# Both attentions' scores computed in row tiles of 64 partitions, rotated keys without a high and a low half, and projection jobs spread over more banks

## What is computed

```
# L0_attn: 16 heads of 8, causal, window 64, relative bias
attn = softmax(q @ k.T * 8**-0.5 + mask + bias);  x = LN(x + (attn @ v) @ w_proj.T + b)
# L0_xattn: 16 heads of 64 over the 512 context tokens
q = (LN(x) @ Wq) per head;  k, v = split(LN(ctx) @ Wkv) per head
k = [k1*cos - k2*sin, k2*cos + k1*sin]            # k1, k2: the two halves of a head's 64 features
attn = softmax(clip(q @ k.T * 64**-0.5, -11, 11)); x = LN(x + (attn @ v) @ Wo + bo)
```

## Time and profile before

| | us |
|---|---|
| Median of 3 runs (1313.61 to 1315.66) | 1315.2 |
| The profiled execution, its own time | 1313.62 |
| Its span | 1311.9 |
| PE busy in the span | 1029.7 (78%) |
| DVE busy | 894.7 (68%) |
| ACT busy | 672.8 (51%) |
| POOL busy | 644.1 (49%) |
| Mean granted TensorE clock | 0.915 |

### The profile page before, as it was taken

One profiled execution on the slowest core, in us unless ns is written; L12 is line 12 of the kernel. 1 busy time (PEld: TensorE's weight loads), 2 busy tenths in 40 slices (PEclk: granted clock), 3 DMA queues, 4 the chain that ended last, 5 costly groups with the idle time before them and its releaser, 6 DMA issues.

```text
span 1311.9 us, 18842 instructions
## 1 busy us (share of the span) xinstructions
PE 1029.7 (78%) x6723; PEld 667.1 (51%) x6723; DVE 894.7 (68%) x2076; ACT 672.8 (51%) x1863; POOL 644.1 (49%) x617
## 2 busy tenths in 40 slices
PE   5667987898888789888888888888865799998321
PEld 3344555556455545645564555455543565564311
DVE  3348877878796797879678877967986200444598
ACT  3746846774784677368557736854521233332000
POOL 1237656755775675567567656756862000111032
PEclk9779999999999999999999999999995899998565
DMA  6000000000000000000000000000000000000301
GB/s 170 1 4 9 1 1 12 1 1 5 8 1 1 12 1 1 1 12 1 1 13 0 1 0 1 1 1 1 1 17 0 1 2 1 8 7 5 33 16 32
DMA packets 56811, 12.78 MB, mean 10 GB/s; under 512 B 40318, under 2 KB 56462, under 8 KB 56590
## 3 DMA queue, kind: packets, MB, share of 16 engines
q1 hardware_dynamic: 56718, 11.58, 4.3%
HBM read 9.46 MB, written 2.12 MB: 9 GB/s over the span
## 4 chain that ended last, share of the span: by engine, by line
PE 39%; DVE 35%; ACT 11%; POOL 10%; issue 4%; DMA 1%; SPq 0%; POOLq 0%; DVEq 0%; ACTq 0%
PE bank_d L1672 6%; PE score_banks L1379 5%; PE bank_a L1360 4%; DVE qm_s L1025 4%; PE score_banks L1736 4%; DVE stats L887 3%; DVE k_sin L1015 3%; PE score_banks L1381 3%; DVE kr_s L1019 3%; PE score_banks L1380 3%; DVE prob L1079 3%; DVE o_rec L1071 2%; PE out_bank L1624 2%; PE score_banks L1402 2%; POOL psum L584 2%
## 5 line engine op out<-in xcount | busy, mean ns | idle before, releaser
L765 ACT ACTIVATE prob<-score_banks 128x512 f32<-128x512 f32 x256 | 152.6, 596 | 105.9 <-PE score_banks L1381 103.3
L505 POOL TENSOR_TENSOR var_eps<-mv,epsilons 128x2 f32<-128x2 f32 (+2 forms) x64 | 12.6, 197 | 390.1 <-DVE mv L890 390.1
L584 POOL TENSOR_TENSOR psum<-psum,prob 128x512 f32<-128x512 f32 x64 | 109.1, 1704 | 120.8 <-DVE prob L1079 120.3
L1379 PE MATMUL score_banks<-qm_s,kr_s 128*128 128x512 f32 x256 | 139.5, 545 | 29.3 <-DVE kr_s L1019 28.9
L1079 DVE TENSOR_SCALAR prob<-prob 128x1024 f32<-128x1024 f32 x128 | 110.4, 862 | 49.7 <-ACT prob L765 49.6
L1559 PE MATMUL out_bank<-prob,v 128*64 128x256 f32 x896 | 115.2, 389 | 1.6 <-DVE on L1072 1.4
L1025 DVE SCALAR_TENSOR_TENSOR qm_s<-q_raw,pair_mask,qm_s 128x256 fp32r<-128x256 f32 x128 | 78.8, 657 | 51.2 <-ACT qm_s L733 51.2
L582 POOL TENSOR_TENSOR psum<-prob 128x512 f32<-128x512 f32 x64 | 92.8, 1449 | 38.3 <-DVE prob L1079 38.3
L1381 PE MATMUL score_banks<-qm_s,kr_s 128*128 128x512 f32 x256 | 108.9, 425 | 0.0
L1380 PE MATMUL score_banks<-qm_s,kr_s 128*128 128x512 f32 x256 | 108.8, 425 | 0.0
L692 ACT ACTIVATE prob<-prob,neg_max 128x128 f32<-128x128 f32 (+1 forms) x256 | 106.2, 421 | 0.0
(11 more groups left out here) (336 smaller groups left out, 2602.0 us busy)
## 6 DMA issues: line engine op xcount, KB each, us to landing
cb<-in_ctx_dram SPq DMA_DIRECT2D x8, 256.0 KB, 2.8
bias_mask<-bias_scratch SPq DMA_DIRECT2D x1, 1536.0 KB, 7.5
xb<-in_x_dram SPq DMA_DIRECT2D x8, 128.0 KB, 2.2
prob<-in_L_xattn_Wkv_dram SPq DMA_DIRECT2D x1, 1024.0 KB, 6.4
att_scratch<-on SPq DMA_DIRECT2D x16, 64.0 KB, 4.1
prob<-att_scratch SPq DMA_DIRECT2D x2, 512.0 KB, 4.0
out_dram<-v SPq DMA_DIRECT2D x4, 256.0 KB, 2.3
prob<-in_L_xattn_Wq_dram SPq DMA_DIRECT2D x1, 512.0 KB, 7.2
```

The lines of the kernel that those rows point to most:

```text
L584: link(g.tensor_tensor(psum[:, p % 2, :], psum[:, p % 2, :], pp[:, 2, :], ALU.add))
L765: s.activation(prob[:, p % 2, kb, :], sc[:, kb % 2, :], ACT.Exp, scale=DH ** -0.5).then_inc(exp_done, 1)
L1379: mm(out_ap, a_high, b_low, start=True, stop=False, **kw)
```

## The change

Seven edits, made together:

1. Cross-attention scores: `kr` and `qh` are plain fp32 tiles; each head's 64 rows are contracted alone, head 0 on partitions 0 to 63, head 1 on 64 to 127, each into a bank of its own. A pair has two units in place of four, both in the same two banks, with one exp of 1024 columns each.
2. Queries are copied once by ACT; the masked copies and both DVE subtractions go.
3. Keys: DVE multiplies the projection in PSUM with `cos_t` into `k_cos`; ACT copies the four 32-row blocks swapped into `k_sin`; POOL multiplies with `sin_t` and adds. `keys_high` and `keys_low` go.
4. Self-attention scores: eight jobs of two heads (h and h+8), 64 rows each, 128 + 192 columns, in `bank_d` and `bank_d2` together; 8 masked copies in place of 16; exp in four groups, after each j.
5. Projection jobs alternate between `bank_p` and `o0_bank` or `bank_d2`.
6. The values and sum of a pair are weighed in the next pair, also over the batch border; output projection, residual and norm of a batch move into the first pair of the next; S_PROJ is split in three slots.
7. `cn_s` and `lat_s` get two buffers, `pt` two in place of four; the context norm's columns are loaded earlier.

```diff
     def unit(u):                                                              # PE
-        split_mm(sc[:, kb % 2, :], kr_s[:, p % 2, 0, c], kr_s[:, p % 2, 1, c], qm_s[:, p % 2, 0],
-                 qm_s[:, p % 2, 1]).then_inc(unit_full, 1)
+        if u == 0:
+            pe.wait_ge(kr_ready, pair + 1)
+            pe.wait_ge(p_free, QUERIES_DONE[pair])
+        if 2 * pair + u >= 1:
+            pe.wait_ge(exp_done, 2 * pair + u)
+        for k in range(2):
+            kb = 2 * u + k
+            for h in range(2):
+                rows_of = slice(DH * h, DH * (h + 1))
+                last = mm(sc[:, h, k * T:(k + 1) * T], kr[rows_of, p % 2, kb * P:(kb + 1) * P],
+                          qh[rows_of, p % 2, :], start=True, stop=True, skip_group_check=True)
+        last.then_inc(unit_full, 1)
...
     if slot in S_SCORE:                                                       # PE, self-attention
-        if i == 0:
-            last = mm(bank[:, 0:4 * P], q0[:, 0:P], km[:, j % 2, :, 0:P], start=True, stop=True)
+        for lo, q, k in ((0, slice(0, P), slice(0, P)), (P, slice(P, T), slice(T - BAND, T))):
+            for half, bank in enumerate((bank_d, bank_d2)):
+                rows_of = slice(DH * half, DH * (half + 1))
+                last = mm(bank[:, lo:lo + k.stop - k.start], q0[rows_of, q], km[rows_of, jj, k], start=True,
+                          stop=True, skip_group_check=True)
...
+    unit(0)                                                                   # PE, one pair
+    prep("keys", prep_keys)
+    slots(0, 1)
+    if pair >= 1:
+        values_of(pair - 1)
+        sum_of(pair - 1)
+    slots(1, 2)
+    unit(1)
+    if p < PAIRS - 1:
+        prep("queries", prep_queries)
+        slots(2, 3)
+        slots(3, 4)
+        prep("values 0", prep_values, 0)
+        slots(4, 5)
+        prep("values 1", prep_values, 1)
+        slots(5, 6)
...
+    if p == 0 and b >= 1:
+        output(b - 1)
...
+def keys(job, key):                                                           # DVE
+    dve.wait_ge(p_full, job.full)
+    if key >= 1:
+        dve.wait_ge(kr_ready, key)
+    w.tensor_tensor(k_cos[:, :], prep_bank[job.bank][:, :], cos_t[:, :], ALU.mult).then_inc(k_cos_ready, 1)
...
+    if (b, p, "keys") in JOB:                                                 # DVE, one pair
+        keys(JOB[b, p, "keys"], pair + 2)
+    clamp(0)
+    slots(0, 1)
+    slots(1, 2)
+    if pair >= 1:
+        attended(pair - 1)
+    clamp(1)
+    slots(2, 3)
...
+def swap_keys(job, key):                                                      # ACT
+    act.wait_ge(k_cos_ready, key + 1)
+    if key >= 1:
+        act.wait_ge(kr_ready, key)
+    bank = prep_bank[job.bank]
+    for block_row in range(4):
+        src, dst = HALF * (block_row ^ 1), HALF * block_row
+        last = s.activation(k_sin[dst:dst + HALF, :], bank[src:src + HALF, :], ACT.Identity)
+    last.then_inc(p_free, 1)
...
+    exps(0)                                                                   # ACT, one pair
+    slots(0, 1)
+    if (b, p, "keys") in JOB:
+        swap_keys(JOB[b, p, "keys"], pair + 2)
+    slots(1, 2)
+    exps(1)
...
+def rotate(key):                                                              # POOL
+    pool.wait_ge(p_free, KEYS_DONE[key])
+    link(g.tensor_tensor(k_sin[:, :], k_sin[:, :], sin_t[:, :], ALU.mult))
+    g.tensor_tensor(kr[:, key % 2, :], k_cos[:, :], k_sin[:, :], ALU.add).then_inc(kr_ready, 1)
...
-S_SCORE = range(10, 22)
-S_EXP = list(range(17, 23)) + list(range(24, 30))
+S_SCORE = (6, 8, 10, 12, 14, 16, 18, 20)
+S_EXP = (range(10, 14), range(14, 19), range(19, 24), range(24, 29))
+S_TURN = (15, 16, 17, 20, 21, 22, 25, 26, 27, 30, 31, 32)
```

More of the change, by code:

```diff
@@ L89, with self_job_before, prep_targets @@
-FIRST_PREP = 5
-SELF_NORMS, NORMS = 5, 6
-UNITS = KB * PAIRS
+def self_job_before(job):
+    if job in (D_Q, D_V):
+        return 0
+    return job
+def prep_targets(p, last):
+    target = {}
+    if p == PAIRS - 1:
+        return {} if last else {"keys": 1, "values 0": 0, "values 1": 0, "queries": 0}
+    if p + 2 < PAIRS or not last:
+        target["keys"] = (p + 2) % PAIRS
+    target["queries"] = p + 1
+    if p % 2 == 1:
+        target["values 0"] = target["values 1"] = (p + 1) // 2
+    return target
@@ new lines, with number_jobs, add @@
+Job = namedtuple("Job", "full bank before done target")
+FIRST_JOBS = {("keys", 0): 0, ("queries", 0): 0, ("values 0", 0): 0, ("values 1", 0): 0, ("keys", 1): 1}
+SECOND_BANK = ("o0", "o0", "o0", None, "d2", "d2", "o0", "o0")
+def number_jobs():
+    jobs, queries_done, keys_done, done, bank, last_of_bank = {}, [], [], 0, None, {}
+    def add(key, kind, target, second):
+        nonlocal bank, done
+        bank = second if second and bank == "p" else "p"
+        done += 1
+        jobs[key] = Job(len(jobs) + 1, bank, last_of_bank.get(bank), done, target)
+        last_of_bank[bank] = jobs[key].done
+        if kind == "queries":
+            queries_done.append(done)
+        if kind == "keys":
+            keys_done.append(done)
+    for (kind, k), target in FIRST_JOBS.items():
+        add((kind, k), kind, target, "o0")
+    for b in range(B):
+        for p in range(PAIRS):
+            for kind, target in prep_targets(p, b == B - 1).items():
+                add((b, p, kind), kind, target, SECOND_BANK[p])
+    return jobs, queries_done, keys_done, done
@@ L92, with last_o0_job @@
+JOB, QUERIES_DONE, KEYS_DONE, ALL_JOBS = number_jobs()
+def last_o0_job(b):
+    return [j.done for key, j in JOB.items() if len(key) == 3 and key[0] == b and key[1] < 3 and j.bank == "o0"][-1]
+SELF_NORMS = 5
+UNITS = 2 * PAIRS
 HALVES = 2 * PAIRS
-SELF_DVE_LINKS, DVE_LINKS, LAST_DVE_LINKS = 6, 16, 10
-SELF_POOL_LINKS, POOL_LINKS, LAST_POOL_LINKS = 13, 38, 23
 Z_FIRST = 512
@@ L786, in batch @@
-                    exps(2)
-                    if not last_pair:
-                        next_values(1)
-                    slots(2, 3)
-                    if not last_pair:
-                        prep(queries, "queries", n(b, PAIRS, p + 2), (p + 1) % 2)
-                    if not (last and last_pair):
-                        keys_high(n(b, PAIRS, p + 2), (p + 1) % 2)
-                    slots(3, 4)
-                    exps(3)
-                    if p + 2 < PAIRS or not last:
-                        prep(keys, "keys", n(b, PAIRS, p + 3))
@@ L798, in batch @@
-                    slots(4, 5)
-                    slots(5, 6)
-                if not last:
-                    for half in range(2):
-                        next_values(half)
-                    prep(queries, "queries", n(b, PAIRS, PAIRS + 1), 0)
+                    if p == PAIRS - 1:
+                        values_job(0)
+                        slots(2, 4)
+                        values_job(1)
+                        slots(4, 6)
+                    if (b, p, "queries") in JOB:
+                        queries(JOB[b, p, "queries"])
@@ L1623, in batch, with output @@
+            for kind, k in FIRST_JOBS:
+                job = JOB[kind, k]
+                if kind == "keys":
+                    prep_keys(job, 0)
+                if kind == "queries":
+                    prep_queries(job, 0)
+                if kind[:6] == "values":
+                    prep_values(job, 0, int(kind[-1]))
+            def output(b):
+                pe.wait_ge(on_ready, n(b, PAIRS, PAIRS))
+                for p in range(PAIRS):
                     for qt in range(QT):
```

679 lines of the change are left out of this document (281 added, 398 removed).

## The result

| | before | after |
|---|---|---|
| Median, us (4 runs each) | 1315.43 | 1271.35 (1269.22 to 1274.2) |
| Ratio, 95% interval | | 0.9667 (0.9641 to 0.9694) |
| Profiled execution, its own time | 1313.62 | 1274.2 |
| Span, mean granted clock | 1311.9, 0.915 | 1272.4, 0.856 |

What follows compares the result with a forecast made beforehand. No single engine was taken as the bound, but a chain from engine to engine, through POOL's adds and rotation in each pair. 1313.6 - 77.4 - 5 + 1.8 + 2.2 = 1235 us, range 1195 to 1285.

Steps and rivals of the forecast that it cites:

- The likeliest case: The summed forecast for the whole kernel: 1235 us, own range 1210 to 1262, a batch of 101.5 to 109; chance 0.62.
- the second case: Each change of tile shape empties PE's array, about 0.16 us each, 5.1 a batch: 110 a batch, 1271 us; chance 0.15.
- -11 per batch, -77.4 for seven: Steady batches: each falls from 116 us to 105, which saves 77.4 us over seven.
- The last batch: Batch without self-attention: pure cycle, six laps of 10.9 and two of 7.2, 80.1 us after 78.35: +1.8.
- That is 18.7, my softest term: What self-attention adds to a batch's cycle: 18.7 us, bounds 0 and 37.7; a share far from it would mean wrong.
- The end, +2.2: From last add to final addition, 7.2 us before: the output matmuls all stand behind the last division, +2.2 us.
- The start, -5: From first keys' projection to first unit, 10.8 us before: product beside copies and earlier exp groups save about 5.
- The lap: One pair's cycle: clamp, POOL's adds and rotation 6.4, product, swap or clamp and division, exp, clamp: 10.9 us a pair.
- the fourth case: A shorter lap: POOL's add and sum fall to 1.3 each, about 98 to 99 a batch, 1193 us; chance 0.12.
- Durations: Single instructions: DVE product 0.7 us, ACT's 1024-column exp 1.04, copy of 32 rows 0.592; DVE busy about 63 a batch.
- Row tiles: Score units on PE: instructions on 64 rows start about 0.126 us apart, so a pair's 16 take 2.0 us.
- the third case: PE's row tiles take turns: 0.23 us an instruction in place of 0.126, 122 a batch, 1355 us; chance 0.08.

Runs made afterwards that it cites:

- Run 11: POOL's third add and rotation put ahead of the norm factors, on the kernel with two rotation buffers and two later norms (1204.7 us): 1255.1 us.
- run 7: Changed kernel plus six unread matmuls on PE ahead of two score jobs a batch and of the last output projection: ratio 0.9679, 1271.4 to 1273.0 us.
- Run 1: Changed kernel with two buffers for `k_cos` and `k_sin`, so product and swap wait for one rotation earlier: 1220.3 us.
- run 4: Changed kernel with the second head's scores computed from the first head's rows, so a unit uses one half of the array: 1331.7 us, one run.
- Run 5: Changed kernel with the eighth pair's values, sum, division, output projection and norm again ahead of the next batch's first unit: 1327.0 us.
- run 2: Changed kernel with the swap's four 32-row copies on ACT made one 128-row copy, halves not swapped: 1232.1 us.

## Why the prediction was right, and where its size was off

The time lies in the range, and the direction was right, but half of the forecast gain did not come: 39.4 us of 78.6. The likeliest case's own range, 1210 to 1262, was missed. The time is inside the stated range, 1195 to 1285, through the place that the second case has in it; that is in part luck. Four terms of the sum were mis-sized; against the profiled executions:

- **"-11 per batch, -77.4 for seven".** This is 33 of the 39 us. The last batch's term runs from eighth pair to eighth pair and so holds the seventh border already. What is left are six such stretches, which gained 696.5 - 652.7 = 43.8, or 7.3 each and not 11 (108.6 a batch, not 105), and the first batch, which has no border ahead of it and gained 1.0 from its first pair's second add (99.39 before, 97.46 after) to its eighth pair's (196.95, 194.00). Seven times 11 became 44.8.
- **"That is 18.7, my softest term".** A batch is 108.6, eight laps of 10.3 are 82.6, so what the self-attention adds is 26, not 18.7, which the prediction itself names as a sign of being wrong (and of its 18.7, 0.3 is rounding: four times 3.5 and four times 1.1 are 18.4). It sits in pairs 0 to 2, which took 5 to 7 us over the lap, not 3.5. The shorter lap gave 4.6 us of this back. I had priced PE's turns and left out DVE's statistics, POOL's factors and ACT's application, one chain through three queues. Run 11 shows that it can hold pair 0; how much of the 26 is its share was not separated.
- **The end, +2.2.** 926.19 to 938.50 is 12.3 us, against 7.2 before: +5.1. Division and `on` are the 2.2 that I booked; the other 2.8 is the projection (6.58 against 3.76), at a granted clock of 0.56 in place of 1.00, behind 2.32 us in which PE waits for the division (run 7 gets 3.73 by filling that time). I had left the clock out on the ground of its 0.97.
- **The start, -5.** It gave 1.9. The last batch 1.1 more, 1.8 forecast (78.35 to 79.48, eighth pair to eighth pair); near by luck, since laps 0.6 shorter than forecast stand beside two of 12 us. The rest behind it is 1.0 longer. Together -1.9 - 1.0 - 43.8 + 1.1 + 5.1 + 1.0 = -39.5; 39.4 is measured.

What held:

- **The lap.** 10.3 for 10.9, its stations in the forecast order. Its POOL part is 5.2 (879.42 to 884.63), not the 6.4 of the earlier trace rows: POOL's add takes 1.27 in every one of 64 pairs, where the earlier trace rows had a median of 1.79. That is half of the fourth case; the other half, a batch of 98, did not come, as the early pairs don't hang on the lap. Run 1 shows lap and coupling by taking the wait away. One reading was wrong: that DVE did not wait for the rotation before the change. It did, through ACT's rounding. In pair 6 of a batch, whose 9.5 us this is, go on:

```profile
542.14 0.64 ACT kr_s L720
542.80 1.76 DVE kr_s L1019
544.56 0.61 DVE prob L1079
...
545.31 1.81 POOL psum L584
```

A lap of 9.46, from 535.85 to 545.31, was there already; now product, swap and exp stand in it where rounding and subtraction stood.

- **Durations.** Product 0.690 (0.7), exp 1.022 (1.039), copy of 32 rows 0.589 (0.592): rows don't count. DVE 62.6 us a batch (63).
- **Row tiles**: 0.133 an instruction for 0.126, and run 4 shows the 0.24 of the third case. The Trainium skill's "TensorE: Matmul & The Clock Gate", Part 3, agrees with the trace on row groups that run at once; for its number of four tiles no run here shows anything.

What was misread or missed:

- **The second case, in the rows.** Its 1271 is the measured time, and its mechanism is in the trace too. I read eight column tiles "on the beat" from their mean of 0.126. Their single starts (the stretch of the earlier trace rows, last two lines below) are two by two at 500.04, 500.30, 500.52 and 500.73, and the transposes begin at 501.05: 0.22 from pair to pair, but 0.32 at the end of the shape. Full-array instructions of another type and the same shape follow without that (506.33, 506.56, then transposes at 506.80). The units are alike, as run 4's lines show: 0.32 in place of 0.22 ahead of a unit and once more behind its first pair, 0.31 at its end, and then 0.34 in place of 0.23 between the first two projections (428.27 to 428.61). So a change of shape costs 0.2 us around a unit and 0.14 to 0.16 where column tiles meet full-array fp32; I had taken 0.16. The Trainium skill's "TensorEngine Tiling (Array Packing)", section "Key Properties", says that changing the tiling mode drains TensorE, and the trace agrees.

```profile
500.73 0.39 PE L1559 MATMUL out_bank<-prob,v 128*64 128x256 f32 x2
501.05 0.33 PE L1360 MATMUL bank_a<-ident,prob 128*128 128x128 f32 x1
```

- **The second case, in the time.** A steady batch has 73 changes of shape in place of 48. By these prices that is 5 to 6 us more of PE's time, an estimate near the case's own 5.1. How much of it lies on the path no run shows. The bare lap above holds no unit, so there it costs nothing. Run 4 adds 13.8 us of PE's time to a batch (0.86 in each of 16 units) and makes it 7.4 longer; at that rate the changes would cost about 3 of the 3.6 us that a batch lies above 105. This is an estimate too, and the self-attention's chains through three queues are its rival for the same 3.6 us.
- **What I did not see** is where the gain came from. My sum set a new batch of 105 against the old one of 116 and never asked in which pairs the 116 stood. Run 5 gives 56 us to the border and minus 12 to the rest, with one rotation buffer, and before, 19.9 and 18.8 us of a batch's 116 stood in two pairs of eight. The distances between the adds of one batch would have told this before any price was worked out; I used only their sum.

Open: what exactly holds pairs 3 to 5 at 13.8, 11.0 and 11.8 in all of the faster versions; run 2's single copy took 0.6 from pair 3, run 4's slower units and run 11's order added to it, and no run shortened the other two. Of the edits other than border and buffers, none was undone alone, the split of S_PROJ included, so its 7.0 us a batch is read from the distances and not shown by a run.

## What to carry to other kernels

List the period of every step of a pipelined loop, not its mean: two steps of 19 us in a batch of eight with a mean of 14.5 are a serial stretch, and emptying that is worth more than shortening the work. When a product moves from one engine to another, draw the lap through its single buffer: here a second buffer was worth 51 us, more than the whole change, and 27 with the border undone. Read single starts before a mean is called a beat: a mean over eight instructions hid the cost of changing the shape. An idle wait and a low clock behind it are one thing; fill the idle time only after looking whether someone waits for what comes after.

## What the runs showed of the hardware

Fp32 matmuls of 256 columns on 64 rows, in different halves of the array, start two by two, 0.22 us from pair to pair; with all on the same half they start singly, 0.22 apart. With the ends of a unit of eight that is 0.133 us an instruction and 0.24. It is all the same whether the halves alternate or come in groups of four instructions (1.06 and 1.07 us for eight). A change of tile shape (full array, column tiles, row tiles) costs 0.14 to 0.2 us: 0.1 ahead of the first instruction of the new shape and 0.05 to 0.1 behind it.

A copy of 512 columns out of PSUM takes ACT 0.59 to 0.60 us for 32, 64 or 128 rows (0.589, 0.592, and 0.597 in run 2), so a swap in four pieces costs four times one.

POOL's add of 128x512 went from a median of 1.79 to 1.27 us. It is not DVE's load as such: before, 56 of the 64 stood beside the product `k_sin` (L1015) and took 1.77 in mean, six with next to nothing beside them 1.27; after, many stand beside DVE's row maxima or norms and all take 1.26 to 1.28. POOL's rotation still takes 1.61 where DVE's `k<-k,keep` runs beside it.

The granted clock of PE was 0.50 behind a wait of 3.8 us inside a batch, and 1.00 in the same place where matmuls filled most of the wait.
